# A stack of bf16 planes in DRAM: seven planes by two writes instead of twelve by six, and twelve narrow loads instead of four

## What is computed

```
xn = layernorm(x)
q, k, v = split(xn @ Wqkv.T); q, k = rope(q), rope(k)
scores = (q @ k.T) / sqrt(8), where 0 <= i - j <= 64
y = softmax(scores) @ v @ Wproj.T + bproj
ffn = sum over the top 2 of 8 experts: w_e * (gelu(xn @ w1[e] + b1[e]) @ w2[e] + b2[e])
out = x + y + ffn
```

## Time and profile before

| | us |
|---|---|
| median of 3 runs | 765.29 |
| lowest and highest | 762.3, 769.11 |
| span of the profiled execution | 707.8 |
| TensorE busy in it | 639.5 (90%) |
| VectorE, ScalarE, GpSimd busy | 480.9, 357.6, 371.5 |
| mean DMA rate | 223 GB/s |

### The profile page before, as it was taken

How to read it: one execution, slowest core, us unless ns; L and a number is a source line. 1 busy time by engine, 2 the same in 40 slices (tenths; PEclk the granted TensorE clock), 3 DMA queues, 4 the chain that set the end, 5 groups by cost and what they waited for, 6 DMA issues and landing times.

```text
span 707.8 us, 26391 instructions
## 1 busy us (share of the span) xinstructions
PE 639.5 (90%) x10175; PEld 515.1 (73%) x10175; DVE 480.9 (68%) x1366; ACT 357.6 (51%) x681; POOL 371.5 (52%) x461
## 2 busy tenths in 40 slices
PE   7677999887989899899989899999999999999885
PEld 3455677655666567666667799999998999996653
DVE  6877797899888688879877344444444444446874
ACT  1354767544556466566556344444444444446552
POOL 1673352246667577777650444545454545453453
PEclk7698999999999999999999999999999999999997
DMA  8578768846878778777687867777777676784988
GB/s 257 180 199 233 207 188 222 221 141 188 252 215 238 218 208 227 217 210 210 193 224 225 249 198 247 237 239 238 242 239 235 225 253 226 251 236 110 312 255 261
DMA packets 156236, 157.92 MB, mean 223 GB/s; under 512 B 20224, under 2 KB 131096, under 8 KB 156112
## 3 DMA queue, kind: packets, MB, share of 16 engines
q1 hardware_dynamic: 141576, 135.29, 66.1%
q0 software_dynamic: 8416, 17.51, 7.2%
q10 hardware_dynamic: 6120, 3.43, 1.8%
HBM read 102.19 MB, written 58.61 MB: 227 GB/s over the span
## 4 chain that ended last, share of the span: by engine, by line
PE 63%; DVE 18%; DMA 8%; issue 6%; SPq 3%; POOL 1%; ACT 0%; ACTq 0%; DVEq 0%
PE ps L762 16%; PE ps L749 15%; DVE mx L1004 7%; PE ps L697 6%; PE ps L632 4%; PE ps L639 3%; PE ps L605 3%; PE ps L681 2%; PE ps L616 2%; DMA QK<-stack 2%; PE ps L725 2%; PE ps L735 2%; PE ps L674 2%; DMA xn<-slots_x 1%; PE ps L567 1%
## 5 line engine op out<-in xcount | busy, mean ns | idle before, releaser
L1298 POOL DMA_INDIRECT chosen_y<-xn,to x135 | 129.2, 957 | 136.4 <-DVE xn L1072 111.3
L1004 DVE TENSOR_REDUCE mx<-ps 128x8 f32<-128x1024 f32 x128 | 156.3, 1221 | 52.4 <-PE ps L639 51.9
L1205 ACT ACTIVATE hb<-ps,xn 128x256 f32<-128x256 f32 x284 | 113.2, 461 | 142.3 <-PE ps L749 142.2
L1183 ACT ACTIVATE PT<-ps 128x1024 f32<-128x1024 f32 x128 | 131.1, 1024 | 88.2 <-PE ps L681 88.1
L1292 POOL DMA_INDIRECT slots_x<-xn,pos x128 | 126.2, 986 | 57.8 <-issue 31.7
L762 PEld LDWEIGHTS ps<-xn,hb 128*128 128x128 f32 x1080 | 131.2, 192 | 3.9 <-ACT hb L1205 0.6
L762 PE MATMUL ps<-xn,hb 128*128 128x128 f32 x1080 | 132.1, 275 | 0.4 <-DVE xn L1066 0.4
L749 PE MATMUL ps<-xn 128*128 128x256 f32 (+1 forms) x568 | 130.1, 372 | 0.0
L749 PEld LDWEIGHTS ps<-xn 128*128 128x128 f32 x568 | 100.2, 192 | 10.3
L697 PE MATMUL ps<-PT,V 128*32 128x64 f32 (+1 forms) x3072 | 86.5, 246 | 1.7 <-ACT Os L1190 1.0
L1066 DVE TENSOR_TENSOR xn<-ps,xn 128x256 f32<-128x256 f32 x71 | 29.1, 410 | 83.3 <-PE ps L762 83.0
(11 more groups left out here) (151 smaller groups left out, 891.9 us busy)
## 6 DMA issues: line engine op xcount, KB each, us to landing
xn<-experts SPq DMA_DIRECT2D x71, 578.0 KB, 3.9
QK<-stack SPq DMA_DIRECT2D x128, 192.0 KB
stack<-sp SPq DMA_DIRECT2D x64, 192.0 KB
xn<-slots_x SPq DMA_DIRECT2D x64, 132.0 KB, 3.4
stack<-sp SPq DMA_DIRECT2D x64, 128.0 KB
xn<-chosen_y SPq DMA_DIRECT2D x32, 256.0 KB, 4.7
stack<-sp SPq DMA_DIRECT2D x64, 64.0 KB
Vc<-values SPq DMA_DIRECT2D x32, 128.0 KB
```

Source lines behind the costliest of these rows:

```text
L1004: e.tensor_reduce(mo[:, :, :, c, t], ps[:, 0:2, :].rearrange("p g (h k) -> p g h k", k=P), AX.X, ALU.max, negate=True).then_inc(v_mx, 1)
L1183: e.activation(PT[:, u % 2, :], ps[:, stb(u):stb(u) + 2, :].rearrange("p c k -> p (c k)"), ACT.Exp, scale=SCALE).then_inc(a_exp, 1)
L1205: e.activation(hb[:, s, c, 0:m], ps[:, 2 * s + c // 2, (c % 2) * SL:(c % 2) * SL + m], ACT.Gelu, bias=b1b[:, i % NW, c:c + 1]).then_inc(a_ ...
L1298: e.indirect_dma_start(out=Ys, out_offset=bass.IndirectOffsetOnAxis(ap=to[:, i % 4, j:j + 1], axis=0), in_=yb[:, i % 4, j, :], in_offset=N ...
```

## The change

`sp` has six parts in one row per partition: third of the query, first and second of the query, first and second of the key, third of the key (slots 0 to 5). Slots 0 to 4 are written as planes 0 to 4 in one transfer, slots 3 and 5 as planes 5 and 6 in a second. No plane is written three times; the first part of the key is there twice. A load takes two neighbouring planes' halves at a time: 16 rows are two planes x eight d. The queries' three pieces start at planes 1, 1, 0, the keys' at 3, 4, 5; with two groups of heads that makes twelve loads of 16 rows of 4 KB. The counts waited for follow: 32 on d_w, 192 on d_r. The pairs of planes multiplied are the same six.

```diff
-    Dst = [nc.dram_tensor(f"stack_{i}", (2, 6, P, 256), bf16).ap() for i in range(3)]
+    Dst = [nc.dram_tensor(f"stack_{i}", (7, P, 256), bf16).ap() for i in range(3)]
...
-        sp = sb("sp", [P, 2, 2, 3, 256], bf16)
+        sp = sb("sp", [P, 2, 6, 256], bf16)
+        FIRSTS, SECONDS, THIRDS = slice(1, 4, 2), slice(2, 5, 2), slice(0, 6, 5)
+
+        QUERIES, KEYS = (1, 1, 0), (3, 4, 5)
...
                     if b >= 3:
-                        e.wait_ge(d_r[(b - 3) % NQ], 64 * ((b - 3) // NQ + 1))
-                    for d0, n in ((0, 3), (3, 2), (5, 1)):
-                        e.dma_start(Dv[0, :, d0:d0 + n, :], sp[:, s, 0, 0:n, :]).then_inc(d_w[b % 3], 16)
-                    for d0, n, s0 in ((0, 3, 0), (3, 2, 1), (5, 1, 2)):
-                        e.dma_start(Dv[1, :, d0:d0 + n, :], sp[:, s, 1, s0:s0 + 1, :].broadcast_to(
-                            (P, n, 256))).then_inc(d_w[b % 3], 16)
+                        e.wait_ge(d_r[(b - 3) % NQ], 192 * ((b - 3) // NQ + 1))
+                    e.dma_start(Dv[:, 0:5, :], sp[:, s, 0:5, :]).then_inc(d_w[b % 3], 16)
+
+                    e.dma_start(Dv[:, 5:7, :], sp[:, s, 3:6:2, :]).then_inc(d_w[b % 3], 16)
...
-                    e.wait_ge(d_w[b % 3], 96 * (b // 3 + 1))
+                    e.wait_ge(d_w[b % 3], 32 * (b // 3 + 1))
                     if b >= NQ:
                         e.wait_ge(e_st, 4 * (b - NQ) + 4)
-                    for i in range(2):
-                        Dv = Dst[b % 3][i].rearrange("s (d h) t -> (s d) (h t)", h=16)
-                        for g in range(2):
-                            e.dma_start(QK[64 * g:64 * g + 48, s, i, :],
-                                        Dv[:, g * 2048:(g + 1) * 2048]).then_inc(d_r[s], 16)
+                    Dv = Dst[b % 3].rearrange("c (d h) t -> (c d) (h t)", h=16)
+                    for g in range(2):
+                        for i, parts in enumerate((QUERIES, KEYS)):
+                            for r, c in zip((0, 16, 32), parts):
+                                e.dma_start(QK[64 * g + r:64 * g + r + 16, s, i, :],
+                                            Dv[8 * c:8 * c + 16, g * 2048:(g + 1) * 2048]).then_inc(d_r[s], 16)
```

More of the change, by code:

```diff
@@ L469, in _ @@
                     s = b % 2
-                    Dv = Dst[b % 3].rearrange("a s c t -> a c s t")
+                    Dv = Dst[b % 3].rearrange("c s t -> s c t")
                     e.wait_ge(p_lo, b + 1)
                     if b >= 3:
-                        e.wait_ge(d_r[(b - 3) % NQ], 64 * ((b - 3) // NQ + 1))
-                    for d0, n in ((0, 3), (3, 2), (5, 1)):
-                        e.dma_start(Dv[0, :, d0:d0 + n, :], sp[:, s, 0, 0:n, :]).then_inc(d_w[b % 3], 16)
-                    for d0, n, s0 in ((0, 3, 0), (3, 2, 1), (5, 1, 2)):
-                        e.dma_start(Dv[1, :, d0:d0 + n, :], sp[:, s, 1, s0:s0 + 1, :].broadcast_to(
-                            (P, n, 256))).then_inc(d_w[b % 3], 16)
+                        e.wait_ge(d_r[(b - 3) % NQ], 192 * ((b - 3) // NQ + 1))
+                    e.dma_start(Dv[:, 0:5, :], sp[:, s, 0:5, :]).then_inc(d_w[b % 3], 16)
+                    e.dma_start(Dv[:, 5:7, :], sp[:, s, 3:6:2, :]).then_inc(d_w[b % 3], 16)
                 elif what == "load":
@@ L623, in _ @@
                     e.wait_ge(p_cb, 1)
-                    e.wait_ge(d_r[s], 64 * (b // NQ + 1))
+                    e.wait_ge(d_r[s], 192 * (b // NQ + 1))
                     if a[0]:
@@ L995, in _ @@
                     e.tensor_tensor(rr[:, b % 2, :].rearrange("p (a t) -> p a t", a=2),
-                                    ps[:, 6, :].rearrange("p (a t) -> p a t", a=2), sp[:, b % 2, :, 0, :],
+                                    ps[:, 6, :].rearrange("p (a t) -> p a t", a=2), sp[:, b % 2, FIRSTS, :],
                                     ALU.subtract).then_inc(v_rr, 1)
@@ L1143, in _ @@
                     if b >= 2:
-                        e.wait_ge(d_w[(b - 2) % 3], 96 * ((b - 2) // 3 + 1))
-                    e.activation(sp[:, b % 2, :, 0, :], ps[:, 6, :].rearrange("p (a t) -> p a t", a=2),
+                        e.wait_ge(d_w[(b - 2) % 3], 32 * ((b - 2) // 3 + 1))
+                    e.activation(sp[:, b % 2, FIRSTS, :], ps[:, 6, :].rearrange("p (a t) -> p a t", a=2),
                                  ACT.Copy).then_inc(a_hi, 1)
@@ L1149, in _ @@
                     e.wait_ge(v_rr, b + 1)
-                    e.activation(sp[:, b % 2, :, 1, :], rr[:, b % 2, :].rearrange("p (a t) -> p a t", a=2),
+                    e.activation(sp[:, b % 2, SECONDS, :], rr[:, b % 2, :].rearrange("p (a t) -> p a t", a=2),
                                  ACT.Copy).then_inc(a_mid, 1)
@@ L1246, in _ @@
                     e.wait_ge(a_mid, b + 1)
-                    e.tensor_tensor(sp[:, b % 2, :, 2, :], rr[:, b % 2, :].rearrange("p (a t) -> p a t", a=2),
-                                    sp[:, b % 2, :, 1, :], ALU.subtract).then_inc(p_lo, 1)
+                    e.tensor_tensor(sp[:, b % 2, THIRDS, :], rr[:, b % 2, :].rearrange("p (a t) -> p a t", a=2),
+                                    sp[:, b % 2, SECONDS, :], ALU.subtract).then_inc(p_lo, 1)
                 elif what == "route":
```

## The result

The changed kernel took 781.26 us (median of 4 runs, 779.24 to 783.12), the kernel before 767.2 beside it; the ratio is 1.018 with a 95% interval of 1.014 to 1.023. The forecast was 785.0 in a range of 760 to 808. Slower it is, by less than the whole 20 us. But the same comparison, made three more times, gave 1.0145, 1.0195 and, in a group of runs where the kernel before takes 714 us and not 767, 1.049 [1.041, 1.056]. What sets the level is open. It isn't simply one chip or another: the record gives the number 6 to the chip of a group at 716 us and to that of a later one at 766 us. The loss depends on the level, and the first profile of before (span 707.8, against timed runs of 762 to 771) belongs to the 716 us level.

A forecast was written before the change was run, and what follows sets the result against it. The prediction took TensorE as busiest and a two-batch lo-write-load circuit as the scatter stage's pace. +3 first stage, +12 scatter stage, +2 start of the experts, +3 last stage made +20 on 765.29 us: 785 us, range 760 to 808.

The forecast's parts named there:

- scatter stage: Attention while scatters run: circuit from 22.6 to 24.2 us, +0.8 a batch over 15 batches, +12 us.
- first stage: Batches 0 to 2: load +3.1, write -1.5, some 0.6 of slack, so +1 each, +3 us.
- early attention: Batches 3 to 10: loads 3.1 us longer against 3.4 us spare, so 0.
- start of the experts: Batch 29's longer load issues delay the slots' load behind them, for which TensorE waits: +2 us.
- the end: Last stage: batch 30's load 3.1 us longer, batch 31's write held 1.5; two thirds counted, +3 us.
- the transfer: Loads into 16 partitions: 0.58 us each, 6.9 for twelve against 3.5 now; 3.1 us added to the group.
- rivals 1 and 2: Narrow loads no slower, hidden behind issue: 763 us, chance 0.22; removed writes decide, landing 2.0 us earlier: 755 us, chance 0.13.
- the issue term: SP's load issues: four take 1.8 us, twelve 5.5, at a median of 0.42 us and 0.04 between.
- two-batch circuit: Scatter stage: scores, scatters, lo, writes, loads, scores again take 22.6 us for two batches, 11.3 each, setting the pace.
- SP's queue: Next write waits 0.7 us behind the loads, but its two issues end at 6.5 instead of 7.8: free.
- Write part: Six issues and twelve planes become two and seven: writes land 1.5 us earlier a batch.
- The 57.5 us: From the profiled span of 707.8 us to the 765.29 median: taken to lie around the span and stay.

The follow-up runs named there:

- before_again: The kernel before, unchanged, run once more for a profile beside the timed runs: 721.36 us, with a span of 719.5.
- the kernel with early writes: Against the kernel before: five writes in place of six, four of them waiting only for ScalarE's mid; loads unchanged. 763.08 us, ratio 0.9955.
- after_again: The changed kernel, unchanged, run again where the kernel before takes 766 us: 775.73 us, ratio 1.0145.
- third group: Runs where the kernel before takes 771 us, repeating the changed kernel (784.27 us, ratio 1.0195) and the one with early writes (771.58 us, ratio 1.000).
- w7_l4_db: Seven planes by two writes and four wide loads, with eight tiny transfers on SP's queue ahead of each batch's loads; against the kernel before 813.64 us, ratio 1.061.
- second group: Runs where the kernel before takes 766 us, with the changed kernel (775.73 us, ratio 1.0145) and the one with early writes (763.08 us, ratio 0.9955).
- w12_l12wide: Against the kernel before: each load of 48 rows cut into three by columns, twelve issues at full width, six writes kept. 778.94 us, ratio 1.093.
- w7_l4_da: Seven planes by two writes and four wide loads, with eight tiny transfers on SP's queue behind each batch's loads; against the kernel before 766.18 us, ratio 0.997.
- w7_l4: The changed kernel's two writes of seven planes, but four loads of 48 rows (wrong planes multiplied); against the kernel before 702.82 us, ratio 0.985.

## Why the prediction was right, and where it wasn't

**Direction and size.** The forecast was made from a profile of the 716 us level and put onto times of the 767 us level. On the timed runs it said +20 us, and +14 came; the direction and the range hold. Part of that is luck: at the level whose profile was read the medians differ by 33 us, which the sum of 20 understates, and at the other the largest term of the sum, the scatter stage, turns out to be nothing (below). Where the loss arises at the 716 us level is told by SP's load starts (before_again, then the changed kernel; starts of batches 13, 28, 29 and 30):

```profile
201.00 3.16 SPq L488 DMA_DIRECT2D QK<-stack  x4
...
372.19 1.73 SPq L488 DMA_DIRECT2D QK<-stack  x4
...
399.47 1.78 SPq L488 DMA_DIRECT2D QK<-stack  x4
...
654.82 1.31 SPq L488 DMA_DIRECT2D QK<-stack  x3
```
```profile
207.97 7.30 SPq L491 DMA_DIRECT2D QK<-stack  x12
...
390.91 6.64 SPq L491 DMA_DIRECT2D QK<-stack  x12
...
421.55 5.48 SPq L491 DMA_DIRECT2D QK<-stack  x12
...
678.02 7.52 SPq L491 DMA_DIRECT2D QK<-stack  x12
```

There are two profiles of the kernel before at this level, with spans of 707.8 and 719.5 us, so each stage has two values (us lost by the changed kernel, whose span is 742.8):

| stage, up to | forecast | against before_again | against the first profile |
|---|---|---|---|
| first stage, batch 3's load | 3 | 0.0 | 2.5 |
| early attention, batch 13's load | 0 | 7.0 | 7.1 |
| scatter stage, batch 28's load | 12 | 11.7 | 14.0 |
| start of the experts, batch 29's load | 2 | 3.4 | 3.1 |
| experts, batch 30's load | 0 | 1.1 | 2.2 |
| the end | 3 | 0.1 | 6.1 |
| sum | 20 | 23.3 | 35.0 |

The pace of the scatter stage, 12.2 us a batch against 11.3 or 11.4, is nearly the forecast's 12.1. The first stage and the end can't be told from the difference between two executions of one kernel. What surely failed is the zero for early attention: 7 us in both columns. That the sum looks right against before_again is no proof of its terms.

**Scatter stage at the 767 us level: nothing.** There is no profile of the kernel before at that level; the kernel with early writes, which takes as long as it within 0.5%, has to stand for it. The changed kernel's batches are 13.9 us apart (after_again, 206.39 to 415.42), and those of the kernel with early writes, which have less to wait for, 14.0 (199.29 to 408.61); in the third group they are 14.1 and 14.0:

```profile
206.39 5.44 SPq L491 DMA_DIRECT2D QK<-stack  x12
...
415.42 6.55 SPq L491 DMA_DIRECT2D QK<-stack  x12
```
```profile
199.29 1.72 SPq L489 DMA_DIRECT2D QK<-stack  x4
...
408.61 1.72 SPq L489 DMA_DIRECT2D QK<-stack  x4
```

Something at that level paces the stage, and seems to take longer than the circuits of either; only w7_l4_db, with 15.0 us a batch (224.07 to 449.03), is slower there. In 170 us, from 200 to 370, TensorE does 3119 matmuls there (early), 3824 at the 716 us level (before_again); it idles inside trains of matmuls that wait for nothing shown. Each window (length, busy us and count of each engine, clock, DMA share, GB/s) is followed by the idle time before the products of the scores in the whole run (us, times; line 640, then 639); the 767 us level first:

```profile
200.00:370.00 170.00, 146.75 (x3119) 99.51 (x3111) 111.25 (x195) 81.36 (x123) 102.57 (x102) 0.97 0.65 176
```
```profile
  issue: 36.5, 81
```
```profile
200.00:370.00 170.00, 156.20 (x3824) 112.63 (x3825) 137.76 (x242) 99.27 (x150) 123.74 (x123) 0.97 0.77 215
```
```profile
  issue: 3.7, 11
```

The loss at that level must then lie outside this stage, and it lies ahead of it. Of the two profiles of the second group, the changed kernel's span is 8.1 us longer than the early one's, and its loads are 7.1 later at batch 13 and 6.8 at batch 28; in the third group the three numbers are 8.8, 9.8 and 10.7. So the stages up to batch 13, to which the forecast gave 3 us, hold nearly all of the loss that was timed.

**The term that was priced wrongly: the transfer.** The forecast priced a load of 64 KB at 0.58 us, for its narrow target. In the changed kernel at the 716 us level, loads and little else move from 38.4 to 43.4 (the window's last two values are DMA share and GB/s):

```profile
38.40:43.40 5.00, 3.51 (x23) 2.37 (x22) 3.86 (x20) 3.02 (x7) 2.88 (x7) 1.00 0.51 134
```

134 GB/s at a share of 0.51, where the earlier trace rows had 227 at 1.03. Half of the time the DMA engines have nothing to do: the issue, one in 0.46 us, is the limit; at a full share it would be some 260 GB/s, an estimate. In this the rivals 1 and 2 were right: the transfer hides behind the issue. The Trainium skill (SBUF — State Buffer, Door 1: the DMA port swizzle) gives 104 GB/s for partitions 0..15, measured at 1 MiB. One such load after another at that rate can't make the window's 134. But a load lands 2.2 us or more after its issue, so several are under way at once, to different partitions, and no run here has the rate into one group of 16 alone. Nor does w12_l12wide: in both kernels the issues set the pace. So the page is neither confirmed nor refuted; its 0.63 us a load, like my 0.58, is not what set the time in this kernel. The 227 GB/s of the earlier trace rows agrees with its 8 ports only roughly: the page has 196 measured for 0..63 and about 218 at most, and the four loads of that window go to both halves of the partitions.

What made the group long all the same is the issue term. Twelve issues should take 5.5 us by the forecast; in the rows shown they take 5.5 once and else 6.1 to 7.5, since single issues are longer than the median (line 491, changed kernel, 716 us level: ns min/median/max):

```profile
L491 SPq DMA_DIRECT2D QK<-stack x384: 302/421/2030, 37.1 to 696.8; - x192
```

That could have been read before: the earlier trace rows has the same 0.42 with a maximum of 2.2 us, and the 32 groups of four in the first profile take 2.1 us on average and not 1.8. Three times that is 6.3; the 32 groups of twelve take 6.5. A median leaves out the few long issues, and a group pays for them.

From first issue to landing seven groups can be followed in the chain of the scatter stage: 8.1 to 9.8 us, 8.9 on average, against 6.2 to 6.6 for four groups of the kernel before. The group grew by some 2.6, where I had 3.1: nearly the right size, and from the issues, not from the transfer. That too is luck.

**The circuit was not the only one.** The forecast took the two-batch circuit of the earlier trace rows, halved, for the pace of the stage. But the chain of the same profile from 198 to 370 us passes through the writes and loads in two rounds only, those ending at 275.4 and 298.0; nearly all the rest is TensorE's and VectorE's own work:

```profile
by line: PE ps L697 13.5%; PE ps L632 9.7%; issue 7.2%; DVE mx L1004 6.9%; PE ps L639 6.4%; DMA QK<-stack 5.9%; PE ps L605 5.6%; PE ps L681 5.3%; PE ps L725 5.1%; PE ps L674 4.5%; DMA stack<-sp 4.5%; PE ps L616 3.8%; PE ps L670 2.8%; SPq L4
```

The chain of the changed kernel has other links (716 us level; start, length):

```profile
282.45 0.26 PE ps L684 x16
...
282.72 0.02 SPq L486
...
282.77 0.32 SPq L491
...
287.11 1.30 SPq L491
...
288.45 0.42 SPq L491
...
288.92 2.18 DMA QK<-stack
...
291.19 0.41 PE ps L635 x4
...
291.82 1.06 PE ps L608 x4
...
293.42 0.23 PE ps L684 x16
```

No write and no `lo` stand in this stretch. SP's load waits until TensorE's scoresT (L684) frees the QK buffer (L486); the twelfth issue ends at 288.87, lands 2.2 later, scores start 0.09 after that, and one iteration further on the next scoresT frees the next buffer: load 20 starts at 293.83. A circuit of one batch, 8.3 us of loads and 2.7 of TensorE, 11.1 us. With the loads of before_again (6.5) it would be 9.2. What SP waited for in the stage, before and after (us, times, longest; windows 201 to 372 and 208 to 391):

```profile
SPq L475 <- POOL sp L1247: 39.9, 15, 7.5
SPq L488 <- DMA stack<-sp: 9.0, 13, 1.9
SPq L484 <- PE ps L681: 6.1, 6, 1.5
```
```profile
SPq L486 <- PE ps L684: 34.9, 14, 4.2
SPq L491 <- DMA stack<-sp: 2.8, 2, 2.3
```

Before, each write waited for `lo`; after, none does, `lo` isn't in the chain of the stage at all, and the loads wait for a free QK buffer instead. So the circuit that the forecast lengthened by 0.8 a batch no longer holds SP. But the one above, with 11.1 us, doesn't explain the 12.2 us a batch alone: eight of the 15 batches take 10.7 to 11.5 us, the other seven 12.3 to 14.3. In three of the 15, batches 13, 22 and 26, the chain goes from the loads through the next write's landing (4.1 to 5.4 us) to the next loads; once, at batch 15, through SP's queue alone. TensorE also works slower after a long wait: its granted clock is 0.50 from 336.5 to 341.3, after batch 23's loads, and four matmuls of line 608 take 2.00 us there instead of 1.06. How the 12 us divide among these was not measured. So the forecast's +12 came about in another way than it said.

That a fifth QK buffer would take this circuit away wasn't tried.

**Early attention.** "3.1 against 3.4 spare: 0" failed: 7 us went there by batch 13's load. The slack was read from one batch, the fifth, and groups aren't equally long. TensorE stands still before the first scores of batches 3 and 6, whose issues take 6.4 and 7.8 us (loads from 70.67 and from 108.67):

```profile
78.96 0.41 PE L635 MATMUL ps<-cb_s 64*64 64x512 bf16 x4 [1.87 <-issue]
...
119.89 0.41 PE L635 MATMUL ps<-cb_s 64*64 64x512 bf16 x4 [1.70 <-issue]
```

Against the two profiles of before the changed kernel's loads are 2.0 and 2.4 us late at batch 4, just behind the first of these waits, and 5.5 and 5.7 us at batch 7, just behind the second. No run was made for it.

**SP's queue.** "That is free" was right for the write: its two issues end no later than its six did, and w7_l4_da shows SP's added time by itself without a loss, at the 767 us level. It wasn't right for everything behind it (changed kernel, 716 us level):

```profile
242.72 1.56 SPq L453 DMA_DIRECT2D Vc<-values  x1
244.32 2.36 SPq L455 DMA_DIRECT2D Vc<-values  x1
246.78 7.07 SPq L491 DMA_DIRECT2D QK<-stack  x12
```

Batch 16's loads start when V's loads leave the queue, with nothing else to wait for.

**Write part.** 1.5 us a batch for the writes: w7_l4 has batches 10.7 us apart in the scatter stage (197.31 to 357.96), 0.7 less than 11.4, which is the half of 1.5 that a two-batch circuit should give, and 13 us in the whole. Against the first profile's 11.3 it is 0.6. This step was right.

**The parts don't add.** At the 716 us level: -1.5% for the writes and +8.5 to +9.1% for the loads alone, +4.9% together. With six writes the twelve loads run into SP's own 13.2 us circuit, which two writes take away.

**The 57.5 us** "around the span" were the difference of the two levels. Around the span lie 1.8 us (783.12 and 781.3).

**The signs named beforehand.** Loads of batches 13 to 28 12.1 us apart: 12.2 at the 716 us level. TensorE waiting 25 us or more for the loads: 19.0. 9 to 10 us from first issue to landing: 8.1 to 9.8. Some 110 GB/s at a full share, and a higher DMA share: neither, 134 at 0.51, and from 200 to 370 us 0.64 against 0.77. The signs of the time came true or nearly so, those of the transfer did not. One sign of being wrong did: issues above 0.46 us, 0.54 on average, and then, as the forecast said, the issue is the term and not the transfer.

## What to carry to other kernels

Count what a group of small transfers costs at the sequencer: here 0.46 us each plus about one long issue in a group of twelve, against which cheaper writes were worth a fifth (13 us of 64). Before pricing a longer load, look for every circuit that it is part of, above all the one through the release of its own buffer; a circuit that is hidden now can be the next bound. And count how often the circuit that you price is on the chain of its stage: two rounds in fifteen batches don't show that it sets the pace. And compare a span with a timed run of the same kernel before adding anything to it; a profile from another level than the timed one has other bounds.

## What was not expected of the hardware

- Two levels: the same kernel takes 714 to 716 us in some groups of runs and 766 to 771 in others. A large part of the difference is in attention with scatters, 11.4 us a batch for 14.0, where TensorE idles inside trains of matmuls. What holds it there is open, and so is whether it goes with the chip.
- Loads into 16 partitions, several under way at once, kept up with one issue in 0.46 us (134 GB/s at a share of 0.51); loads of the same bytes into 48 partitions cost the same (ratios 1.091 and 1.093).
- Single issues on SP's queue take 1.3 us and up to 2.2 instead of 0.42, in groups of four and of twelve, for wide and narrow loads alike. The cause is open.
- Eight tiny transfers moved from behind to ahead of four loads made 6.4% of time.
